# A two-block model step on one core: query copy, x store, scaling, Hadamard rounding and FFN banks put in other places

## The chip, the cores and the metric

The kernel runs on one core of a Trainium2 chip. The time is that of one execution on the device in microseconds (us); a run gives one such time, and the median of three runs is used.

## The reference

The input x is 4 x 512 tokens of 512 channels; a second tensor f has the same shape, cond is 4 x 128. Twice, with other constants (w, u), a tensor is scanned along the tokens (this goes by tile of 128 channels of one batch element):

```
a[t] = a[t-1] * decay + exp(min(f,30)) * f      (forwards and backwards)
b[t] = b[t-1] * decay + exp(min(f,30))
y = sigmoid(x) * num / max(den, 1e-8) * (0.8 + 0.2 * tf)
```

The first y feeds a segmented attention of 16 heads: q, k, v = y @ Wq, Wk, Wv (512 x 2048 each); per head and segment of 128 tokens a causal softmax attention, joined with a read from a memory matrix that a delta rule updates from segment to segment; then x = x + att @ Wo. The second y (from this new x) feeds a gated network: `hidden = silu(y @ W1) * (y @ W3)`, 2048 wide, a Walsh-Hadamard transform of hidden, and `x = x + hidden @ W2`. Everything is fp32.

## The kernel before

Channels lie on partitions, tokens in the free dimension. Products with weights are made from a high and a low part of each operand (fp32r): `three` (L543 to L548) issues three matmuls, high x high, high x low, low x high. A weight of 128 x 1024 enters in two halves through `stage`; ScalarE (L1366) or GpSimd (L1774) rounds it to the high part `wh`, GpSimd (L1776) or VectorE (`low_o`, L1041) subtracts for the low part `wl`. `weight_stream` sets the order of all weights, and six ring slots hold them. The second and later uses of the attention weights fetch the saved parts from memory.

Five engines run five programs written out by hand, `tensor`, `vector`, `scalar`, `gpsimd` and `sync`, which wait for each other through counting semaphores. An engine takes its program strictly in its order. Attention is a loop of 32 steps `n` (`NN`): a batch element times a pair of heads. In step n TensorE does in this order: `turn_k` (L665, transposed keys), `scores` (L677, into banks X[0], X[1]), `turn_att(n-1)` (L731), the value projection of step n+1 (`v_part`, into G[0], G[1]) with `update` and `recall` of the memory (L694, L702, L703, in Z) between, `turn_p` (L712), the key and query projections of step n+1 (`kq_part`, G), and `pv` (L722). Every fourth step from 4 on is a burst: it also applies Wo to the attention of four steps (`wo`, 8 weights), and `add_wo` (L1131) adds it into `xb`.

ScalarE copies what TensorE leaves in the banks: `copy_kq` (L1524) with `relu_kq` and `minus_exp` for keys and queries, `copy_kn` (L1557), the softmax exponentials `exp_s` (L1564), `copy_v` (L1549), `copy_pt` (L1572), `high_att` (L1581). `scores(n)` waits for both query copies of step n; the second of them, `copy_kq(n, "q", 1, G[1])`, stands at the head of ScalarE's step n. The first matmul of the key projection of head j waits for `copy_v` of half j (`a_v`), because it writes the bank from which the values are copied. `update(n, 1)` waits for `delta` and `t2` of VectorE's `recalled`.

Between this work each engine runs `behind(n, k)`, eight places per step, whose steps a table (`shared_out`, with the costs in `SCAN`, `HADAMARD` and `MODULATE`) hands out: the scans of later tiles (EK, EU, ER, yh on ScalarE; NF, DF, NBK, DBK and others on VectorE; EKV, EUV, ER, yl on GpSimd), and from step 23 on the transform of W2. The transform takes eight parts i: VectorE's levels in `HA`/`HB` (L989, L990), the rounding `HH` by ScalarE (`high_w2`, L1440), the rest `HL` by VectorE (`low_w2`, L995), two pairs of matmuls into X[0], X[1] (`hadamard`, L742 and L743, which wait for both and for the copies of part i-1), and the copies to `HO` by ScalarE (`out_w2`, L1458) with a store (L1460).

`keep_x1(b)` stores the finished `xb` of a batch element to `x1_s`, by four transfers of 256 KB from ScalarE's queue (L1601), in steps 9, 17 and 25 and once at the end. `fetch_x(b)` (L1989) on SyncE waits for it and loads the next element into `xb`. SyncE also issues all weight transfers, in order.

`scale_v` (L1839) on GpSimd multiplies the values of the next step; `split_w` is its weight splitting.

At the end of attention the network's units begin: 32 units `u` (`ffn`), each with a gate and a linear product of two heads j. `bank_of(u, k)` gives their banks: X for j = 0, G for j = 1; unit 0 is done inside step 31 in G[0], G[1]. VectorE's `gate` (L1137, L1142) frees a bank. Unit 1 stands between `turn_att(31)` and the last `wo(7)`:

```
            turn_att(NN - 1)
            w.wait_ge(v_jn, 8 * NN)
            up(1, 0, "1", bank_of(1, 0))
            up(1, 0, "3", bank_of(1, 1))
            for dc in range(NC):
                wo(7, dc)
```

`turn_att(n)` waits for `join(n, 3)` of VectorE (L1099, pT).

Of the kernel before, what the change touches and what calls it, by code (L numbers as in the profile page):

```python
# [238 lines left out]
def adaln_attn_ffn(nc, xT_d, fT_d, cond_d, wu_d, wq_d, wk_d, wv_d, wo_d, betas_d,  # L239
# [9 lines left out]
    with ExitStack() as ctx:  # L249
# [267 lines left out]
        def bank_of(u, k):  # L517

            return [X[0], X[1], G[0], G[1]][k]
# [22 lines left out]
        def tensor(e):  # L542
# [92 lines left out]
            def wo(m, dc):  # L635

                if dc == 0:
                    w.wait_ge(a_at, 8 * m + 8)
                    w.wait_ge(v_al, 8 * m + 8)
                if dc >= 2:  # L640
                    w.wait_ge(v_xb, 4 * m + dc - 1)
                elif m < 7:
                    w.wait_ge(a_v, 2 * (4 * m + 5) + dc - 1)
                else:
                    w.wait_ge(v_f3, 2)
                for half in range(2):
                    at = PLACE["o", 8 * m + 2 * dc + half]
                    hi, lo = ring(at)
                    wait_split(w, at)
                    for r in range(8):  # L650
                        cols = slice(128 * r, 128 * r + 128)
                        k = three(G[dc % 2][:, 0:256], hi[:, cols], lo[:, cols], ah[:, 8 * half + r, :],
                                  al[:, 8 * half + r, :], half == 0 and r == 0, half == 1 and r == 7)
                    k.then_inc(pe_o, 1)
# [120 lines left out]
            for n in range(NN):  # L775
# [56 lines left out]
                if burst:  # L832
                    kq_part(nx, "k", 1, 0)
                    kq_part(nx, "k", 1, 1)
                    for j in range(2):
                        kq_part(nx, "q", j, 0)
                        kq_part(nx, "q", j, 1)
                elif more:
                    kq_part(nx, "q", 0, 1)
                    kq_part(nx, "q", 1, 0)  # L840
                    kq_part(nx, "q", 1, 1)
            turn_att(NN - 1)
            w.wait_ge(v_jn, 8 * NN)
            up(1, 0, "1", bank_of(1, 0))
# [35 lines left out]
        def vector(e):  # L880
# [244 lines left out]
            def add_wo(m, dc):  # L1125
                b, half = m // 2, m % 2
                w.wait_ge(pe_o, 8 * m + 2 * dc + 2)
                w.wait_ge(d_xb[b], 16 if b == 0 else 64)
                src = G[dc % 2][:, 0:256].rearrange("p (h s r) -> p h s r", h=8, s=4)
                dst = xb[:, dc, :].rearrange("p (s h r) -> p h s r", s=4, h=16)[:, 8 * half:8 * half + 8]  # L1130
                e.tensor_tensor(dst, dst, src, ALU.add).then_inc(v_xb, 1)  # L1131
# [217 lines left out]
        def scalar(e):  # L1349
# [121 lines left out]
            def behind(n, k):  # L1471
                for name, i, _ in STEPS[at[0]:UPTO[n, k]]:
# [13 lines left out]
                    elif name == "hi":  # L1486
                        high_w2(i)
                    elif name == "load":
                        load_w2(i)
                    elif name == "mult":  # L1490
# [7 lines left out]
            def behind_ffn(u, k):  # L1498
                for name, t, _ in FSTEPS[late[0]:FUPTO.get((u, k), late[0])]:
# [10 lines left out]
                    elif name == "zh":  # L1510
                        w.wait_ge(v_zt, 4 * b + c + 1)
                        w.wait_ge(v_xb, 32)
                        w.wait_ge(d_x1[3], 64)
# [84 lines left out]
            def keep_x1(b):  # L1598
                w.wait_ge(v_xb, 8 * b + 8)
                for dc in range(NC):  # L1600
                    e.dma_start(x1_s[b, :, dc, :], xb[:, dc, :]).then_inc(d_x1[b], 16)  # L1601
# [54 lines left out]
            for n in range(NN):  # L1656
# [3 lines left out]
                if n > 0:  # L1660
                    copy_kq(n, "q", 1, G[1])
# [10 lines left out]
                if n > 1 and is_burst(n - 1) and (n - 1) // 4 % 2 == 0:  # L1672
                    keep_x1((n - 1) // 8 - 1)
# [21 lines left out]
                copy_pt(n)  # L1695
                if not more:
# [19 lines left out]
                if more:  # L1716
# [3 lines left out]
                    split_hi(here + (14 if burst else 6))  # L1720
                else:
# [33 lines left out]
        def gpsimd(e):  # L1755
# [104 lines left out]
            for n in range(NN):  # L1860
# [17 lines left out]
                if more:  # L1878
                    scale_v(nx)
                if burst:  # L1880
                    split_w(here + 11)
                behind(n, 6)
# [28 lines left out]
        def sync(e):  # L1911
# [53 lines left out]
            def z_load(b):  # L1965

                w.wait_ge(d_rs[b], 64)
                w.wait_ge(d_x1[b], 64)
# [17 lines left out]
            def fetch_x(b):  # L1986
                w.wait_ge(d_x1[b - 1], 64)
# [63 lines left out]
            def load_x(b):  # L2051
                w.wait_ge(d_x1[b], 64)
# [6 lines left out]
            def load_z(t):  # L2059
                if t < NT:  # L2060
                    _, b, c = TILES[t]
                    w.wait_ge(d_x1[b], 64)
# [92 lines left out]
```

## Time and profile before

| | us |
|---|---|
| median of 3 runs (1629.97 to 1631.04) | 1630.14 |
| the profiled execution, its own time | 1630.78 |
| its span | 1629.0 |
| TensorE busy | 1573.5 |
| VectorE busy | 1160.8 |
| ScalarE busy | 742.8 |
| GpSimd busy | 559.8 |

The profile is one execution. A row of the timeline gives start, duration, engine, line, operation, output<-inputs and shape; merged rows carry the number of instructions (x4) and the time of all. In brackets stands the idle time of the engine before it and what ended it. PE is TensorE's matmul, PEld its weight load, DVE VectorE, ACT ScalarE, POOL GpSimd, SP SyncE; ACTq and SPq are DMA issues of these. PEclk is the clock granted to TensorE as a share of full speed.

### The profile page before, as it was taken

How to read it: one execution, taken by the hardware profiler on the slowest of the kernel's cores; microseconds unless marked ns; L12 is line 12 of the kernel's file. 1: busy time of each engine (PE TensorE's matmuls, PEld its weight loads, DVE VectorE, ACT ScalarE, POOL GpSimd, SP SyncE). 2: the span in 40 equal slices, each digit the busy share in tenths (PEclk: the TensorE clock that was granted, in tenths of full speed). 3: DMA queues.
4: the chain of work that ended last, by engine and by line, in shares of the span. 5: the costliest groups of instructions: out<-in, count | busy, mean ns of one | idle time of the engine just before them, and what ended most of it. 6: DMA issues, size and time to landing. Idle time of an engine off the chain costs nothing.

```text
span 1629.0 us, 26858 instructions
## 1 busy us (share of the span) xinstructions
PE 1573.5 (97%) x9656; PEld 1396.4 (86%) x9656; DVE 1160.8 (71%) x2688; ACT 742.8 (46%) x1627; POOL 559.8 (34%) x408
## 2 busy tenths in 40 slices
PE   3799999999999999999999999999999999999999
PEld 2589989999999999999998899889888888888887
DVE  8988978888888878788765773666888884333333
ACT  3456556535635526536445653553554442222221
POOL 1665656242232122231102000134655553433431
PEclk9999999999999999999999999999999999999999
DMA  5356575595474475474477457238212214211101
GB/s 172 116 201 207 203 277 204 201 350 199 142 288 142 149 276 191 150 261 157 147 267 277 167 189 277 85 120 284 72 52 91 60 38 144 70 58 39 52 13 53
DMA packets 111252, 262.30 MB, mean 161 GB/s; under 512 B 11408, under 2 KB 36368, under 8 KB 110224
## 3 DMA queue, kind: packets, MB, share of 16 engines
q1 hardware_dynamic: 90240, 227.27, 39.3%
q10 hardware_dynamic: 20880, 33.31, 6.5%
q8 instruction: 78, 1.28, 0.3%
q14 instruction: 54, 0.44, 0.1%
HBM read 212.29 MB, written 48.25 MB: 160 GB/s over the span
## 4 chain that ended last, share of the span: by engine, by line
PE 84%; DVE 10%; issue 2%; ACT 2%; DMA 1%; ACTq 1%; DVEq 0%; SPq 0%
PE psG L546 16%; PE psG L548 16%; PE psG L547 16%; PE psX L722 3%; PE psX L547 3%; PE psX L546 3%; PE psX L548 3%; PE psX L677 3%; PE psZ L703 3%; PE psZ L694 2%; PE psZ L702 2%; PE psZ L547 2%; PE psY L547 2%; PE psZ L548 2%; PE psY L548 2%
## 5 line engine op out<-in xcount | busy, mean ns | idle before, releaser
L1776 POOL TENSOR_TENSOR wl<-stage,wh 128x512 fp32r<-128x512 f32 x160 | 226.4, 1437 | 166.2 <-ACT wh L1366 163.8
L546 PE MATMUL psG<-yh,wh 128*128 128x512 f32 x632 | 257.8, 408 | 4.4 <-ACT v L1549 2.5
L548 PE MATMUL psG<-yh,wl 128*128 128x512 f32 x632 | 247.6, 392 | 0.0
L547 PE MATMUL psG<-yl,wh 128*128 128x512 f32 x632 | 247.0, 391 | 0.0
L1839 POOL TENSOR_TENSOR vs<-v,omb 128x512 f32<-128x512 f32 x64 | 97.2, 1540 | 275.1 <-PE psX L722 272.0
L1846 POOL TENSOR_TENSOR hl<-sg,hh 128x512 fp32r<-128x512 f32 x64 | 86.4, 1350 | 220.6 <-ACT hh L1615 220.6
L546 PE MATMUL psG<-ah,wh 128*128 128x256 f32 x512 | 144.7, 283 | 1.1 <-DVE wl L1041 1.1
L547 PE MATMUL psG<-al,wh 128*128 128x256 f32 x512 | 142.9, 279 | 0.0
L548 PE MATMUL psG<-ah,wl 128*128 128x256 f32 x512 | 142.9, 279 | 0.0
L546 PE MATMUL psG<-wh,yh 128*128 128x256 f32 x480 | 142.0, 296 | 0.0
L546 PEld LDWEIGHTS psG<-yh,wh 128*128 128x128 f32 x632 | 119.5, 189 | 25.9 <-issue 3.2
L548 PEld LDWEIGHTS psG<-yh,wl 128*128 128x128 f32 x632 | 118.8, 188 | 26.1
L547 PEld LDWEIGHTS psG<-yl,wh 128*128 128x128 f32 x632 | 119.5, 189 | 20.1
L548 PE MATMUL psG<-wh,yl 128*128 128x256 f32 x480 | 136.1, 283 | 0.0
L547 PE MATMUL psG<-wl,yh 128*128 128x256 f32 x480 | 136.0, 283 | 0.0
L1366 ACT ACTIVATE wh<-stage 128x512 fp32r<-128x512 f32 x152 | 87.8, 622 | 91.6 <-PE psZ L548 29.0
L1615 ACT ACTIVATE hh<-sg 128x512 fp32r<-128x512 f32 x64 | 40.5, 632 | 174.6 <-DVE sg L1142 174.6
L1524 ACT ACTIVATE kT<-psG 128x512 f32<-128x512 f32 x62 | 37.0, 597 | 156.5 <-PE psG L548 156.5
L969 DVE RECIPROCAL DBK<-DF 128x128 f32<-128x128 f32 x120 | 107.3, 925 | 0.6
L1564 ACT ACTIVATE S<-S,st 128x128 f32<-128x128 f32 x256 | 99.1, 389 | 18.7 <-issue 13.9
L1051 DVE CUSTOM_DVE_ANT_0 S<-psX,mask 128x128 f32<-128x128 f32 x256 | 59.2, 286 | 57.6 <-PE psX L677 57.4
L546 PEld LDWEIGHTS psG<-ah,wh 128*128 128x128 f32 x512 | 96.3, 188 | 1.3 <-ACT wh L1366 1.2
(213 smaller groups left out, 4203.3 us busy)
## 6 DMA issues: line engine op xcount, KB each, us to landing
wh<-high_o SPq DMA_DIRECT2D x52, 512.0 KB, 3.5
wl<-low_o SPq DMA_DIRECT2D x52, 512.0 KB, 4.6
stage<-in_w SPq DMA_DIRECT2D x64, 256.0 KB, 4.3
wh<-high_k SPq DMA_DIRECT2D x23, 512.0 KB, 3.7
wl<-low_k SPq DMA_DIRECT2D x23, 512.0 KB, 4.8
wh<-high_q SPq DMA_DIRECT2D x23, 512.0 KB, 3.9
wl<-low_q SPq DMA_DIRECT2D x23, 512.0 KB, 5.6
wh<-high_v SPq DMA_DIRECT2D x22, 512.0 KB, 4.1
```

Source lines behind the costliest of these rows:

```text
L546: e.matmul(out, lh, rh, start=first, stop=False, skip_group_check=check)
L547: e.matmul(out, lh, rl, start=False, stop=False, skip_group_check=check)
L548: return e.matmul(out, ll, rh, start=False, stop=last, skip_group_check=check)
L677: m = e.matmul(X[j][:, seg(s)], qT[:, j, seg(s)], kT[:, j, seg(s)], start=True, stop=True)
L703: e.matmul(Z[j][:, 129:258], sq[:, j, seg(s)], mem[:, j, 0:P + 1], start=True, stop=True).then_inc(pe_am, 1)
L969: e.reciprocal(dbk[:, 128 * j:128 * j + 128], df[:, 128 * j:128 * j + 128]).then_inc(v_rc, 1)
L1051: m = e.tensor_tensor_reduce(S[:, j, seg(s)], X[j][:, seg(s)], mask[:, :], 1.0, NEG, ALU.add, ALU.max, st[:, 0, j, s:s + 1])
L1366: e.activation(hi, raw, ACT.Copy).then_inc(a_wh, 1)
L1564: m = e.activation(S[:, j, seg(s)], S[:, j, seg(s)], ACT.Exp, bias=st[:, 1, j, s:s + 1], scale=SCALE, accum_out=st[:, 2, j, s:s + 1])
L1776: e.tensor_tensor(lo, raw, hi, ALU.subtract).then_inc(p_wl, 1)
L1839: e.tensor_tensor(vs[:, :, j, :], v[n % 2][:, :, j, 0:P], omb[:, 128 * j:128 * j + 128].rearrange("p (a d) -> p a d", a=1).to_broadcast([P ...
L1846: e.tensor_tensor(hl[u % 2][:, j, :], hid(k)[:, :], hh[u % 2][:, j, :], ALU.subtract).then_inc(p_hl, 1)
```

## The change

It makes six edits.

- The copy of the second query head for step n+1 moves on ScalarE from the head of step n+1 to the end of step n, ahead of `behind(n, 7)`.
- `keep_x1` stores a batch element by one transfer of 1024 KB, not four, and in steps 9, 17 and 25 it stands behind `copy_pt`, not ahead of the softmax exponentials. All waits for `d_x1` count 16.
- In step 4 GpSimd's `scale_v` stands behind the splits of the weights up to `here + 11`.
- The part 7 of the transform of W2 is rounded (`high_w2(7)`) ahead of the copies `out_w2(6)` in step 30.
- Network units use G for j = 0 and X for j = 1. TensorE issues unit 1's first product into G[0] ahead of `turn_att(31)` and waits for `v_f1` there, for `v_f3` ahead of the second product.
- The last `wo(7)` and `add_wo(7)` use X.

```diff
--- before.py
+++ after.py
@@ -516,7 +516,7 @@
 
         def bank_of(u, k):
 
-            return [X[0], X[1], G[0], G[1]][k]
+            return [G[0], G[1], X[0], X[1]][k]
 
         def hid(k):
 
@@ -642,14 +642,14 @@
                 elif m < 7:
                     w.wait_ge(a_v, 2 * (4 * m + 5) + dc - 1)
                 else:
-                    w.wait_ge(v_f3, 2)
+                    w.wait_ge(v_jn, 8 * NN)
                 for half in range(2):
                     at = PLACE["o", 8 * m + 2 * dc + half]
                     hi, lo = ring(at)
                     wait_split(w, at)
                     for r in range(8):
                         cols = slice(128 * r, 128 * r + 128)
-                        k = three(G[dc % 2][:, 0:256], hi[:, cols], lo[:, cols], ah[:, 8 * half + r, :],
+                        k = three((G if m < 7 else X)[dc % 2][:, 0:256], hi[:, cols], lo[:, cols], ah[:, 8 * half + r, :],
                                   al[:, 8 * half + r, :], half == 0 and r == 0, half == 1 and r == 7)
                     k.then_inc(pe_o, 1)
 
@@ -839,9 +839,10 @@
                     kq_part(nx, "q", 0, 1)
                     kq_part(nx, "q", 1, 0)
                     kq_part(nx, "q", 1, 1)
+            w.wait_ge(v_f1, 2)
+            up(1, 0, "1", bank_of(1, 0))
             turn_att(NN - 1)
-            w.wait_ge(v_jn, 8 * NN)
-            up(1, 0, "1", bank_of(1, 0))
+            w.wait_ge(v_f3, 2)
             up(1, 0, "3", bank_of(1, 1))
             for dc in range(NC):
                 wo(7, dc)
@@ -1126,7 +1127,7 @@
                 b, half = m // 2, m % 2
                 w.wait_ge(pe_o, 8 * m + 2 * dc + 2)
                 w.wait_ge(d_xb[b], 16 if b == 0 else 64)
-                src = G[dc % 2][:, 0:256].rearrange("p (h s r) -> p h s r", h=8, s=4)
+                src = (G if m < 7 else X)[dc % 2][:, 0:256].rearrange("p (h s r) -> p h s r", h=8, s=4)
                 dst = xb[:, dc, :].rearrange("p (s h r) -> p h s r", s=4, h=16)[:, 8 * half:8 * half + 8]
                 e.tensor_tensor(dst, dst, src, ALU.add).then_inc(v_xb, 1)
 
@@ -1485,9 +1486,11 @@
                         keep_ratio(i)
                     elif name == "hi":
                         high_w2(i)
+                        if i == 7:
+                            out_w2(6)
                     elif name == "load":
                         load_w2(i)
-                    elif name == "mult":
+                    elif name == "mult" and i != 6:
                         out_w2(i)
                     elif name == "zsig":
                         z_sigmoid(i)
@@ -1510,7 +1513,7 @@
                     elif name == "zh":
                         w.wait_ge(v_zt, 4 * b + c + 1)
                         w.wait_ge(v_xb, 32)
-                        w.wait_ge(d_x1[3], 64)
+                        w.wait_ge(d_x1[3], 16)
                         e.activation(zh[b][:, c, :], ZS[t % 2][:, :], ACT.Copy).then_inc(a_zh, 1)
                 late[0] = FUPTO.get((u, k), late[0])
 
@@ -1597,8 +1600,7 @@
 
             def keep_x1(b):
                 w.wait_ge(v_xb, 8 * b + 8)
-                for dc in range(NC):
-                    e.dma_start(x1_s[b, :, dc, :], xb[:, dc, :]).then_inc(d_x1[b], 16)
+                e.dma_start(x1_s[b], xb[:, :, :]).then_inc(d_x1[b], 16)
 
             def sigmoid(u, j, bank):
                 k = 2 * u + j
@@ -1657,8 +1659,6 @@
                 nx, burst = n + 1, is_burst(n)
                 more = nx < NN
                 here = PLACE["v", nx] if more else PLACE["1", 0]
-                if n > 0:
-                    copy_kq(n, "q", 1, G[1])
                 copy_kn(n)
                 if n == 0:
                     copy_v(1, 0)
@@ -1669,8 +1669,6 @@
                     load_beta(n)
                 if more:
                     load_ombeta(nx)
-                if n > 1 and is_burst(n - 1) and (n - 1) // 4 % 2 == 0:
-                    keep_x1((n - 1) // 8 - 1)
                 behind(n, 0)
                 exp_s(n, 0)
                 split_hi(here + 3)
@@ -1693,6 +1691,8 @@
                 if burst:
                     split_hi(here + 6)
                 copy_pt(n)
+                if n > 1 and is_burst(n - 1) and (n - 1) // 4 % 2 == 0:
+                    keep_x1((n - 1) // 8 - 1)
                 if not more:
                     sigmoid(0, 1, G[0])
                 behind(n, 4)
@@ -1718,6 +1718,7 @@
                     copy_kq(nx, "q", 0, G[0])
                     exp_kq(nx, "q", 0, G[0])
                     split_hi(here + (14 if burst else 6))
+                    copy_kq(nx, "q", 1, G[1])
                 else:
                     high_h(0, 0)
                     high_h(0, 1)
@@ -1875,10 +1876,12 @@
                 behind(n, 4)
                 split_w(here + (9 if burst else 5))
                 behind(n, 5)
-                if more:
+                if more and n != 4:
                     scale_v(nx)
                 if burst:
                     split_w(here + 11)
+                if n == 4:
+                    scale_v(nx)
                 behind(n, 6)
                 if burst:
                     split_w(here + 13)
...
@@ -1984,7 +1987,7 @@
                 at[0] = UPTO[n, k]
 
             def fetch_x(b):
-                w.wait_ge(d_x1[b - 1], 64)
+                w.wait_ge(d_x1[b - 1], 16)
                 for dc in range(NC):
                     e.dma_start(xb[:, dc, :], xT_d[b, :, dc, :]).then_inc(d_xb[b], 16)
```

The other places with `d_x1` change in the same way.

ScalarE in step 25, from the load of the one-minus-betas to the copies of pT (x_s is the store of `xb`, S the exponentials, HO and HH the transform of W2, v the values), before:

```order
L1595 DMA omb<-beta_s 128x256
L1601 DMA x_s<-xb 128x512 x4
L1564 ACTIVATE S,st<-S,st 128x128 x8
L1458 ACTIVATE HO<-psX 128x512 x2
L1460 DMA w_s<-HO 128x1024
L1549 ACTIVATE v<-psG 128x4x128
L1440 ACTIVATE HH<-HA 128x1024
```

and now, with the copies of pT and the store that follows them:

```order
L1598 DMA omb<-beta_s 128x256
L1567 ACTIVATE S,st<-S,st 128x128 x8
L1459 ACTIVATE HO<-psX 128x512 x2
L1461 DMA w_s<-HO 128x1024
L1552 ACTIVATE v<-psG 128x4x128
L1441 ACTIVATE HH<-HA 128x1024
L1451 DMA HA<-in_w 128x1024
L1552 ACTIVATE v<-psG 128x4x128
L1575 ACTIVATE pT<-psY 128x512 x2
L1603 DMA x_s<-xb 128x2048
```

The four stores ahead of the exponentials are one store behind the copies of pT.

ScalarE in step 30, from the exponentials on, before:

```order
L1564 ACTIVATE S,st<-S,st 128x128 x8
L1458 ACTIVATE HO<-psX 128x512 x2
L1460 DMA w_s<-HO 128x1024
L1549 ACTIVATE v<-psG 128x4x128
L1440 ACTIVATE HH<-HA 128x1024
```

and now:

```order
L1567 ACTIVATE S,st<-S,st 128x128 x8
L1552 ACTIVATE v<-psG 128x4x128
L1441 ACTIVATE HH<-HA 128x1024
L1459 ACTIVATE HO<-psX 128x512 x2
L1461 DMA w_s<-HO 128x1024
```

The value copy and the rounding HH stand ahead of the two copies to HO and their store.

TensorE at the end of step 31 (mem is the memory, pT the joined attention), before:

```order
L703 MATMUL psZ<-mem,sq 128x129 x2
L731 MATMUL psY<-ident,pT 128x128 x8
L546 MATMUL psX<-yh,wh 128x512
L547 MATMUL psX<-yl,wh 128x512
L548 MATMUL psX<-yh,wl 128x512
```

and now (the first dots stand for three more such triples, those at the end for the second product in psG, which the last `wo` in psX follows):

```order
L703 MATMUL psZ<-mem,sq 128x129 x2
L546 MATMUL psG<-yh,wh 128x512
L547 MATMUL psG<-yl,wh 128x512
L548 MATMUL psG<-yh,wl 128x512
...
L731 MATMUL psY<-ident,pT 128x128 x8
L546 MATMUL psG<-yh,wh 128x512
...
```

Twelve matmuls of unit 1 stand between the last read of the memory and the last transposes.

## Rows read from the trace of the kernel before

**Rows 1.** The page, busy time by engine.
```profile
PE 1573.5 (97%) x9656; PEld 1396.4 (86%) x9656; DVE 1160.8 (71%) x2688; ACT 742.8 (46%) x1627; POOL 559.8 (34%) x408
```

**Rows 2.** TensorE's waits: engine, tile, line, releaser, us in total, times, longest.
```profile
PE psX L568 <- DVE oys L975: 28.6, 4, 22.5
...
PE psX L677 <- issue: 1.8, 1, 1.8
PE psG L546 <- DVE wl L1041: 1.1, 1, 1.1
```

**Rows 3.** Timeline, step 17: ScalarE's stores, TensorE's first key matmul.
```profile
616.90 2.94 ACTq L1601 DMA_DIRECT2D x_s<-xb  x4
...
624.23 0.47 PE L546 MATMUL psG<-yh,wh 128*128 128x512 f32 x1 [1.30 <-ACT v L1549]
```

**Rows 4.** Timeline, step 25: the same, and TensorE's memory update.
```profile
875.75 2.82 ACTq L1601 DMA_DIRECT2D x_s<-xb  x4
...
883.99 0.47 PE L546 MATMUL psG<-yh,wh 128*128 128x512 f32 x1 [1.15 <-ACT v L1549]
...
887.18 0.72 PE L694 MATMUL psZ<-delta,kn 128*128 128x129 f32 x4 [0.69 <-DVE t L1083]
```

**Rows 5.** Timeline, step 30: the transform's last two parts on three engines.
```profile
1042.87 1.06 ACT L1458 ACTIVATE HO<-psX 128x512 f32<-128x512 f32 x2
...
1044.33 0.60 ACT L1549 ACTIVATE v<-psG 128x512 f32<-128x512 f32 x1 [0.40 <-ACT HO L1458]
1044.82 1.05 ACT L1440 ACTIVATE HH<-HA 128x1024 fp32r<-128x1024 f32 x1
...
1045.90 1.22 DVE L995 TENSOR_TENSOR HL<-HA,HH 128x1024 fp32r<-128x1024 f32 x1 [3.44 <-ACT HH L1440]
...
1047.22 0.47 PE L742 MATMUL psX<-HH,had 128*128 128x512 f32 x1 [1.86 <-issue]
```

**Rows 6.** Stretches: busy us by engine (count), PEclk, DMA share, GB/s.
```profile
228.10:231.60 3.50, 3.50 (x31) 3.50 (x32) 3.40 (x20) 2.72 (x6) 3.33 (x4) 1.00 1.04 412
...
1048.60:1052.00 3.40, 3.40 (x15) 3.11 (x14) 0.00 (x0) 1.05 (x2) 0.91 (x1) 0.51 0.47 175
1091.00:1096.00 5.00, 5.00 (x24) 4.14 (x24) 1.98 (x3) 2.04 (x4) 1.29 (x1) 1.00 0.33 105
```

**Rows 7.** Timeline, end of step 31.
```profile
1080.64 5.80 POOL L1805 TENSOR_TENSOR yl<-zr,yh 128x512 fp32r<-128x512 f32 x4 [17.22 <-ACT yh L1469]
...
1090.01 1.09 PE L731 MATMUL psY<-ident,pT 128*128 128x128 f32 x8 [1.16 <-DVE pT L1099]
1090.13 0.68 DVE L1142 TENSOR_TENSOR sg<-psG,sg 128x512 f32<-128x512 f32 x1
```

**Rows 8.** Timeline, step 4: VectorE's low parts beside GpSimd's scaling.
```profile
200.04 3.00 POOL L1839 TENSOR_TENSOR vs<-v,omb 128x512 f32<-128x512 f32 x2 [1.86 <-PE psX L722]
...
200.51 3.09 DVE L1041 TENSOR_TENSOR wl<-stage,wh 128x512 fp32r<-128x512 f32 x2
...
205.16 2.48 DVE L1041 TENSOR_TENSOR wl<-stage,wh 128x512 fp32r<-128x512 f32 x4
```

**Rows 9.** Timeline, head of step 5, ScalarE and VectorE.
```profile
227.39 0.58 ACT L1524 ACTIVATE qT<-psG 128x512 f32<-128x512 f32 x1
...
234.57 0.48 DVE L1065 TENSOR_TENSOR mem<-psZ,mem 128x129 f32<-128x129 f32 x2
```

**Rows 10.** DMA issues by line: count, KB each, median us from issue to landing.
```profile
x<-x_s SPq DMA_DIRECT2D x4, 1024.0 KB, 6.6
```

**Rows 11.** Timeline, SyncE in step 9: the fetch, and the next weight.
```profile
371.23 2.50 SPq L1989 DMA_DIRECT2D xb<-in_xT  x4
376.72 0.33 SPq L1950 DMA_DIRECT2D wh<-high_k  x1
```

**Rows 12.** Timeline, ScalarE and TensorE at the head of step 17.
```profile
613.07 0.87 ACT L1557 ACTIVATE kn<-psY 128x384 f32<-128x384 f32 x2
...
614.82 0.82 PE L731 MATMUL psY<-ident,pT 128*128 128x128 f32 x6
```

More of the change, by code:

```diff
@@ L1967, in z_load @@
                 w.wait_ge(d_rs[b], 64)
-                w.wait_ge(d_x1[b], 64)
+                w.wait_ge(d_x1[b], 16)
                 w.wait_ge(pe_q, 2 * NG * (3 + b))
@@ L2051, in load_x @@
             def load_x(b):
-                w.wait_ge(d_x1[b], 64)
+                w.wait_ge(d_x1[b], 16)
                 if b >= 2:
@@ L2061, in load_z @@
                     _, b, c = TILES[t]
-                    w.wait_ge(d_x1[b], 64)
+                    w.wait_ge(d_x1[b], 16)
                     wait_attention(w)
```

## The prediction

> **What bounds the kernel now.** I read the page first: TensorE's matmuls are busy for 1573.5 of 1629.0 us [rows 1]. That leaves 55.5 us in which it stands still, and no edit here changes what it computes (the count of matmuls is the same). So the change can only be worth stalls of TensorE, and every other engine counts only where TensorE waits for it. The second view is the list of TensorE's waits [rows 2]. The largest, 28.6 us, is the opening, before the scans have given a first tile; nothing in the change touches it. What is left to win are single waits of 0.7 to 1.9 us, each in one step. I went through them in the timeline and asked of each which edit ends it, and what is late next.
>
> **Part by part.**
>
> The x store. ScalarE's queue issues four transfers in 2.94 us in step 17 [rows 3] and in 2.82 us in step 25 [rows 4], and the exponentials, the HO copies and the value copy `v` stand behind them in its order. TensorE's first key matmul may not write the bank before `v` is out of it, and idles 1.30 us [rows 3] and 1.15 us [rows 4] for it. In step 25 HH is behind `v` too, VectorE's HL behind HH, VectorE's `recalled` behind HL, and so the memory update idles 0.69 us more [rows 4]. With the stores behind `copy_pt` all of it comes 2.8 to 2.9 us earlier, more than each wait, so all three go: 1.30 + 1.15 + 0.69 = 3.14 us. Bounds: 0 if something else is late at the same place, 3.14 if nothing is. I take 3.14, since what else the first key matmul needs (weights, TensorE's own order) was there long before. One store is now issued while ScalarE copies pT and waits for the next key projection: cost nothing. In step 9 the store stood in the same place, and no wait of TensorE shows there: worth nothing. The last store, at the end of attention, is followed by network work that TensorE has queued: nothing.
>
> The last rounding. In step 30 ScalarE does the two HO copies of part 6 (1042.87) and issues their store, then `v` at 1044.33, then HH at 1044.82, then VectorE HL at 1045.90, and TensorE's Hadamard matmul starts at 1047.22 after 1.86 us of idle time [rows 5]. The change puts `v` first: it starts at 1042.87, and everything in the chain v, HH, HL, matmul comes 1044.33 - 1042.87 = 1.46 us earlier. The HO copies end then behind HH, at about 1045.4, still ahead of HL's end (1047.12 - 1.46 = 1045.7), so HL remains what comes last. Gain 1.46, idle time left 0.40.
>
> The clock. Behind that stall the granted clock is 0.51 of full speed, the 1.2 GHz level, from 1048.6 to 1052.0; after the stall of 1.8 us at the head of step 5 [rows 2] it stayed at 1.00 [rows 6]. The engine lost at most half of 3.4 us, 1.7 us; less, because a few weight loads and small matmuls do not run at the array's pace. I take 1.5 (bounds 0, if the level drops for another reason, and 1.7): a stall of 0.40 is far below every one that was followed by full speed. The Trainium skill's page "TensorE: Matmul & The Clock Gate", section "Why this matters for your kernels", warns only of idle gaps between matmul bursts that are longer than this one; by it the stall would not be the cause, the slow stretch could stay, and the sum would lose this term. The row, with 0.51 right behind the longest stall that I found in steps 4 to 31, speaks for the stall. This disagreement is a rival below.
>
> The second unit. TensorE's last transposes idle 1.16 us for pT [rows 7]. Now twelve matmuls of unit 1 stand ahead of them, whose bank G[0] is free since the gate of unit 0 and whose last input, `yl`, is done at 1080.64 + 5.80 = 1086.44 [rows 7]. In the next stretch 24 such matmuls, the first and the last in part, fill 5.0 us [rows 6], so twelve last some 2.7 us, more than the 1.16, which goes whole. What comes next: the second product needs the gate that starts at 1090.13 and lasts 0.68 us [rows 7]; it starts at 1090.01 - 1.16 = 1088.85, plus 2.7 and some 0.9 for the transposes: 1092.4, later than 1090.8. `wo(7)` needs the copies and low parts of both transposes, about 1.8 us behind them, and 2.7 us of matmuls cover that. Swapping X and G in all later units changes nothing: the waits are the same. Gain 1.16 (bounds 0 and 1.2).
>
> The scaling in step 4. GpSimd's `scale_v` runs from 200.04 to 203.04, and beside it VectorE's two low parts take 3.09 us; four of the same later take 2.48 us, 0.62 each [rows 8]. TensorE waits 1.1 us for the slower ones [rows 2]. Without the neighbour they take 1.24 and the wait goes.
>
> The query copy, with it. At the head of step 5 the second query copy starts at 227.39, behind a scan exponential that waits for VectorE, and the scores idle 1.8 us [rows 2, 9]. Ahead of it, the copy starts as soon as the projection ends, some 2.5 us earlier. But TensorE's next need of VectorE is the memory add at 234.57 [rows 9], on which the next read of the memory follows at once, and VectorE is busy for 3.40 of 3.50 us in the stretch behind the stall [rows 6]; it has no idle time by which it could come earlier. So TensorE, 1.8 us earlier, waits the 1.8 us there. These two edits together are worth what VectorE gains by step 5. It gains at most 3.09 - 1.24 = 1.85 us in step 4, but the moved scaling now runs beside its scans and key sums before step 5 and takes some of it back. Bounds: 0, and 1.1 + 1.8 = 2.9. I take 0.9, near the lower wait. In the other steps where scan work stood ahead of the query copy (12 of them) the copy waited for the projection anyway.
>
> What the query copy costs. In these steps one scan operation of 0.6 to 0.7 us now runs behind the copy, not while ScalarE waits for TensorE, and `copy_kn` comes later by so much. In step 17 it lasts until 613.94, and `turn_att` that waits for it starts at 614.82 [rows 12]: 0.88 us of cover, enough for 0.7. Only in step 24 (HH and a small copy, some 1.3 us) is it used up; half of the two copies is enough for the first transposes, and I put 0.1 us there, within the rounding.
>
> Sum: 3.14 + 1.46 + 1.5 + 1.16 + 0.9 = 8.16 us. The profiled execution's own time is 1630.78, so 1622.6. It stands 0.64 above the median of 1630.14, and each wait that goes whole gives a little more than its idle time, since the profile counts it from a modelled end of the matmul before. I therefore forecast **1622.0 us**, 0.5% faster. A measurement of this kernel can tell about 0.2%, 3.3 us, from no change: 1626.9 is the border.
>
> **Rivals.**
>
> - The clock falls in another place, or the level was not bound to the stall (the page's reading): 8.16 - 1.5 = 6.7 us, 1623.5. For it: one occurrence is thin evidence, and a stall of 1.8 us left the clock alone. Chance 0.15.
> - Step 5 gives back its stall whole, because VectorE runs ahead without its neighbour: 2.0 us more, 1620.0. Against it: VectorE's row of work without a pause. Chance 0.10.
> - The moved scan operations land on TensorE's path. If the cover of 0.88 us [rows 12] is used up elsewhere, each of 12 steps costs up to 0.6: 7 us, 1629.2, no difference that can be told. It decides once an operation is longer than the cover. Against it: the operations that I see are shorter. Chance 0.07.
> - Slower: the single store. Landing took 6.6 us for 1024 KB in the median [rows 10]. In step 9 SyncE fetches the next element at 371.23 and issues a key weight at 376.72 [rows 11]. A store issued behind `copy_pt` shortly before, at 370, and landing 6.6 us later, or 10 us (half as much again, for other traffic), would let the fetch start at 376.6 to 380, and its four issues of 2.50 us [rows 11] put the weight at 379.1 to 382.5, up to 5.8 us late; three times 5.8 on TensorE's path is 17.4 us: 1639.4. It decides where a weight is used within that time of its issue. Against it: this weight goes into a slot of six that is read two steps (52 us) later. Chance 0.03.
> - The change does not do what it says: the order of the instructions shows each move. Half of the stalls return for reasons that I do not see: 1626.0, chance 0.05.
>
> My forecast has 0.60.
>
> **How the numbers follow.** The range takes in the first two rivals and the bounds of the terms: low 1619.5 (2.9 in place of 0.9, and 0.5 of run to run), high 1625.5 (no clock term, and 2 us of stalls that return). It leaves out the third, fourth and most of the last, 0.15 in all. Faster by over 0.2%: 0.60 + 0.15 + 0.10 + 0.03 = 0.88; slower by over 0.2%: 0.03; the rest, 0.09, is within 0.2%.
>
> **What would show it.** In the profile after: TensorE's waits for v in steps 17 and 25 and for t2 in step 25 are gone; the Hadamard matmul of step 30 idles some 0.4 us and no stretch of half clock follows it; the last transposes do not idle; the wait of 1.1 us in step 4 is gone, and that of 1.8 us in step 5 is no longer at the scores but at `copy_kn` and at the memory read, 0.9 us less in sum over steps 4 and 5. The forecast is wrong if a wait for weights or for `copy_kn` appears in many steps, or if TensorE's idle time falls by less than 4 us.

## The result, and the profile after

The changed kernel takes **1621.1 us** (median of 4 runs, 1620.47 to 1621.25); the kernel before took 1630.59 in the same session (4 runs). The ratio is 0.994, 95% interval 0.9925 to 0.9954. That is 9.5 us or 0.6% faster; the forecast was 1622.0, from 1619.5 to 1625.5.

The page of the changed kernel, span and busy time by engine:

```profile
span 1619.3 us, 26845 instructions
...
PE 1570.0 (97%) x9656; PEld 1393.9 (86%) x9656; DVE 1157.1 (71%) x2688; ACT 742.8 (46%) x1627; POOL 560.2 (35%) x408
```

The number of matmuls is the same, and TensorE stands still for 49.3 us in place of 55.5 [rows 1]. It is also busy for 3.5 us less, with the same work. A third profile of the kernel before, shown below, whose clock fell nowhere that it cost, is busy for 1571.5 us; so some 2.0 of the 3.5 us are the clock, and the rest may be idle time that the modelled ends of the matmuls hide. TensorE's waits in the changed kernel (tile, line, releaser: us in total, times, longest):

```profile
PE psX L568 <- DVE oys L976: 30.9, 4, 22.7
PE psZ L702 <- DVE mem L1066: 5.1, 5, 2.2
PE psZ L703 <- DVE mem L1066: 3.1, 7, 0.5
PE psG L546 <- DMA wl<-low_q: 1.8, 1, 1.8
PE psY L731 <- ACT kn L1560: 1.7, 1, 1.7
...
PE psX L742 <- DVE HL L996: 0.4, 1, 0.4
```

Against the list of before [rows 2]: gone are the waits for `v` (steps 17 and 25), for the low part in step 4, for pT at the end of attention, and the 1.8 us at the scores of step 5. The Hadamard matmul of step 30 idles 0.4 us. New is a wait of 1.7 us for `kn`, and the wait for low_q, a weight of step 8 that the change does not touch, is 1.8 us (1.3 before).

For the account I cut TensorE's trace at the first matmul of each step's scores. In all fourteen profiles of this document a step's length repeats within 0.06 us in most steps; steps 0, 4, 5, 8, 17, 25 and 30 and the stretch from 31 on do not repeat so well, and once (in the second profile of the kernel before) step 24 took 0.87 us more. For these steps several profiles are needed. The steps that differ, in the first profiles of both kernels (us):

```
step                 before    after    less by
0                     28.36    26.64     1.72
4 and 5               79.17    78.82     0.35
8                     50.29    50.77    -0.48
17                    27.84    26.32     1.52
25                    30.35    28.01     2.34
30                    31.78    28.77     3.01
31 to the last matmul 557.43  556.11     1.32
```

The other steps add 0.1 us, and the first scores come 0.17 us later; the sum is the 9.7 us of the spans. Nothing was forecast for the first row and the third.

In step 30 VectorE's HL and TensorE's Hadamard matmul follow the rounding at once (ScalarE, changed kernel):

```profile
1037.47 0.58 ACT L1552 ACTIVATE v<-psG 128x512 f32<-128x512 f32 x1
1037.94 1.05 ACT L1441 ACTIVATE HH<-HA 128x1024 fp32r<-128x1024 f32 x1
1038.89 1.06 ACT L1459 ACTIVATE HO<-psX 128x512 f32<-128x512 f32 x2
```

`v` has no idle time ahead of it now, and the HO copies run beside HL; before, they stood ahead of both [rows 5].

At the end of attention twelve matmuls stand ahead of the last transposes, which start without an idle time (TensorE, first and last of the twelve):

```profile
1080.16 0.48 PE L546 MATMUL psG<-yh,wh 128*128 128x512 f32 x1
...
1082.75 0.39 PE L548 MATMUL psG<-yh,wl 128*128 128x512 f32 x1
1082.98 1.03 PE L731 MATMUL psY<-ident,pT 128*128 128x128 f32 x8
```

### The profile page after: what moved, and what is told of

Same layout as the page of the kernel before. It is cut to its first block, busy times and chain, and to the rows that moved or that the text cites. A ratio compares the mean times of both kernels' runs of the same rounds, so it can differ in the third digit from the quotient of the medians.

```text
span 1619.3 us, 26845 instructions
## 1 busy us (share of the span) xinstructions
PE 1570.0 (97%) x9656; PEld 1393.9 (86%) x9656; DVE 1157.1 (71%) x2688; ACT 742.8 (46%) x1627; POOL 560.2 (35%) x408
## 4 chain that ended last, share of the span: by engine, by line
PE 85%; DVE 10%; issue 2%; DMA 2%; ACT 1%; SPq 0%; POOL 0%; ACTq 0%; DVEq 0%; POOLq 0%
PE psG L546 15%; PE psG L548 15%; PE psG L547 15%; PE psX L546 3%; PE psX L547 3%; PE psX L548 3%; PE psX L722 3%; PE psX L677 3%; PE psZ L703 3%; PE psZ L694 2%; PE psZ L702 2%; PE psZ L548 2%; PE psZ L547 2%; PE psY L547 2%; PE psY L548 2%
## 5 line engine op out<-in xcount | busy, mean ns | idle before, releaser
L546 PE MATMUL psG<-ah,wh 128*128 128x256 f32 x448 | 126.7, 283 | 0.0
L547 PE MATMUL psG<-al,wh 128*128 128x256 f32 x448 | 125.1, 279 | 0.0
L548 PE MATMUL psG<-ah,wl 128*128 128x256 f32 x448 | 125.1, 279 | 0.0
L546 PEld LDWEIGHTS psG<-wh,yh 128*128 128x128 f32 x480 | 91.6, 191 | 0.3
```

What stands on the lines that cost most here:

```text
L546: e.matmul(out, lh, rh, start=first, stop=False, skip_group_check=check)
L547: e.matmul(out, lh, rl, start=False, stop=False, skip_group_check=check)
L548: return e.matmul(out, ll, rh, start=False, stop=last, skip_group_check=check)
```

## Experiments

### The query copy and the scaling

Three variants of the changed kernel: the query copy back at the head of the step (first edit), the scaling back ahead of the splits (second), and both. Their expectations follow in this order.

```diff
+                if n > 0:
+                    copy_kq(n, "q", 1, G[1])
                 copy_kn(n)
...
-                    copy_kq(nx, "q", 1, G[1])
```

```diff
-                if more and n != 4:
+                if more:
                     scale_v(nx)
                 if burst:
                     split_w(here + 11)
-                if n == 4:
-                    scale_v(nx)
```

> The changed kernel with the second query copy back at the head of the step. In the changed kernel step 5 has two stalls of TensorE, 1.7 us at the last transposes for copy_kn and one at the memory read (1.3 us longer from start to start than without a wait). Theory: both are set by VectorE's unbroken row of work, so the copy's place is worth nothing there: with it back the scores of step 5 wait some 1.8 us, the memory read waits again as long as in the changed kernel or less, and the scores of step 6 start within 0.3 us of the changed kernel's 252.0 us. In all other steps nothing moves. Time 1621 +- 0.5, unless the half-clock stretch of the opening falls elsewhere (1.7 us). Rival: the query copy is worth its wait; the scores of step 6 then start 1 us or more later, 1622.5.

> The changed kernel with GpSimd's scaling of step 4 back ahead of the splits. Theory: the wait of 1.1 us for the low part in step 4 returns, and step 5 gives most of it back, since VectorE then works without its neighbour there: steps 4 and 5 together are 0.2 to 0.6 us longer than in the changed kernel, and of that step 8's wait for the weight low_q takes the rest, since that weight's landing hangs on transfers. Time 1621.1 to 1621.7. Rival (as I forecast it for the two edits): 0.9 us or more stay, 1622.0.

> The changed kernel with both of these undone. Theory: steps 4 and 5 are 0.35 us longer in sum (the difference of the two traces), step 8's wait for low_q is 0.5 us shorter again, so that from step 9 on the two edits together are worth nothing: 1621.1 +- 0.4 at the same opening. If the opening's half-clock stretch comes from the moved query copy it returns to 79 us and costs 1.7: 1622.8. Rival: the two edits are worth the 0.9 that I forecast, 1622.0, with step 9's start 0.9 later.

Measured: 1619.72 us (1619.24 to 1620.58), 1623.09 (1620.27 to 1624.78) and 1621.38 (1620.56 to 1622.5), beside 1629.62 for the kernel before (14 runs, 1626.93 to 1632.23). The second lies above both its theory and its rival, but its five runs spread over 4.5 us, and its profiled run took 1620.49. With such a spread the medians cannot tell a microsecond, and the steps are the better witness:

```
us                  step 4   step 5    sum    step 8
before               50.48    28.69   79.17    50.29
both back            50.48    28.67   79.15    50.29
scaling back         50.46    28.71   79.17    50.00
query copy back      48.94    29.60   78.54    50.09
changed              49.15    29.67   78.82    50.77
```

The query copy is worth nothing here: with it back the sum is not longer. The wait only changes its place. With the copy late, the scores wait 2.7 us and the memory read not at all; with it early, `kn` takes 1.7 us and the memory read the rest. Two lines of TensorE's waits, with the copy back:

```profile
PE psZ L702 <- DVE mem L1066: 3.9, 4, 2.2
PE psX L677 <- issue: 2.7, 1, 2.7
```

The memory read's waits sum to 3.9 us, where the changed kernel has 5.1. VectorE's row of work sets the end of both, so I had the mechanism right and the size of the first wait too small (1.8 expected).

The scaling is worth 0.35 us in the pair of first profiles and 0.6 between the last two variants. Over all profiles of this document it is 0.6: with the scaling moved, steps 4 and 5 last 78.03 to 78.82 us (eight profiles, mean 78.48), without 78.84 to 79.17 (six, mean 79.11). In step 4 it gives all that was forecast: the two low parts that took 3.09 us beside GpSimd [rows 8] take 1.29 us now (first row below), the four behind them 2.59 (2.48 before), and the step is 1.3 to 1.8 us shorter. But the scaling now falls beside VectorE's key sums of step 5 (VectorE and GpSimd, changed kernel):

```profile
198.91 1.29 DVE L1042 TENSOR_TENSOR wl<-stage,wh 128x512 fp32r<-128x512 f32 x2
...
201.75 2.59 DVE L1042 TENSOR_TENSOR wl<-stage,wh 128x512 fp32r<-128x512 f32 x4
```

```profile
217.26 2.72 DVE L1123 SCALAR_TENSOR_TENSOR sk<-kT,etmp 128x512 f32<-128x512 f32 x2
```

```profile
214.94 3.48 POOL L1840 TENSOR_TENSOR vs<-v,omb 128x512 f32<-128x512 f32 x2
218.36 1.08 POOL L1796 TENSOR_SCALAR ER<-ER 128x512 f32<-128x512 f32 x1
```

One such sum takes 0.68 us without a neighbour, two would be 1.36; they took 2.72, the first beside the scaling, the second beside the operation behind it, and step 5 is 0.7 to 1.0 us longer.

Step 8, with its wait for low_q, is not tied to these edits: it lasted 49.80 to 50.77 us in all profiles, both ways (the last version below, which moves that weight, left out). And step 0 lasted 26.6 us in all three variants, also with the copy back; the changed kernel's gain of 1.72 us there is not the query copy's.

### The rounding alone

The kernel before with this single edit:

```diff
                         high_w2(i)
+                        if i == 7:
+                            out_w2(6)
...
-                    elif name == "mult":
+                    elif name == "mult" and i != 6:
                         out_w2(i)
```

> The kernel before with the last rounding ahead of the copies as the only change. Theory: the Hadamard matmul of step 30 idles some 0.4 us in place of 1.86, and the stretch of half clock behind it is gone: 1630.6 - 1.46 - 1.5 = 1627.6, and step 30 lasts 28.8 us (31.8 before). Rival (the level of the clock does not hang on that stall): the half-clock stretch stays somewhere in steps 29 to 31, 1629.1, step 30 or its neighbour 30.3 us.

1626.93 us (10 runs, 1625.5 to 1627.99), beside 1629.62: ratio 0.9984, interval 0.9974 to 0.9993. The median gain, 2.7 us, is near the theory's, but the profile shows that not all went as the theory has it. Step 30 lasts 30.07 us, there is no stretch of half clock, and the Hadamard matmul still idles 1.7 us. ScalarE was held up at another place, by the issue of a small load ahead of the exponentials:

```profile
1036.93 1.75 ACTq L1597 DMA_DIRECT2D omb<-beta_s  x1
```

At the same place the issue took 0.44 us in the kernel before and 0.45 in the changed kernel. So this profile has a stall of the old length without the drop of the clock. That put in doubt that the stall is what takes the clock down, and the next three kernels are for that.

### Stalls of other lengths, and the clock

The changed kernel with the rounding back behind the copies, and with one or two more copies of HA ahead of the rounding:

```diff
+                if i == 7:
+                    for m in range(2):
+                        e.activation(HH[:, :], HA[i % 2][:, :], ACT.Copy).then_inc(a_had, 1)
+                        w.wait_ge(a_had, m + 2)
                 e.activation(HH[:, :], HA[i % 2][:, :], ACT.Copy).then_inc(a_h, 1)
```

> The changed kernel with the last rounding of the W2 transform back behind the copies. The stall ahead of the Hadamard matmul in step 30 is some 1.85 us again, in a kernel where everything else is the changed one. Theory (a stall so long takes the clock down): half clock behind it, step 30 lasts 31.8 us, 1624.1. Rival, for which the run with the rounding alone spoke (a stall of 1.7 us and no half clock): the level does not hang on the length of this stall, step 30 lasts 30.2 us, 1622.6.

> The changed kernel with one more copy of HA to HH (1.05 us, and a wait for it) ahead of the rounding of part 7, which makes the stall ahead of the Hadamard matmul 1.5 us in place of 0.4. Both theories: no half clock (the stalls of 1.7 and 1.8 us had none), step 30 lasts 29.9 us, 1622.2.

> The same with two more copies: a stall of 2.6 us. Theory (length decides, somewhere above 1.7 us): half clock behind it, 1.5 to 1.7 us on top, step 30 lasts 32.5 to 32.7 us. Rival (length does not decide alone): none, step 30 lasts 31.0 us.

1621.33 us (1620.78 to 1623.29), 1622.02 (1621.54 to 1625.68) and 1623.23 (1622.56 to 1625.51), beside 1630.25 for the kernel before (13 runs). The stalls ahead of the Hadamard matmul were 1.9, 2.7 and 3.3 us (the small load's issue took 1.70 us in the second and 1.21 in the third), step 30 lasted 30.27, 31.11 and 31.73 us, and no half clock followed in any of them. With the longest:

```profile
1042.30 0.47 PE L742 MATMUL psX<-HH,had 128*128 128x512 f32 x1 [3.33 <-DVE HL L996]
```

```profile
1042.00:1045.40 3.40, 3.10 (x19) 2.86 (x20) 1.44 (x7) 1.92 (x4) 2.29 (x2) 1.00 0.38 154
```

The third figure from the right is the granted clock, 1.00. So the length of the stall alone does not decide. The Trainium skill's page "TensorE: Matmul & The Clock Gate", section "Why this matters for your kernels", asks for no idle gaps of TensorE above about 3 us, or the level falls. The rows here do not agree with it: a stall of 3.33 us, just above that figure, left the level alone, and behind one of 1.86 us [rows 5, 6], well below it, the level fell.

### The kernel before, two more profiles

> The kernel before once more, for a second profile. So far its one profile has a half-clock stretch behind the stall of 1.86 us in step 30, and none of the four variants with stalls of 1.7 to 3.3 us at that place has one. Theory (a stall there makes the drop possible, and chance decides where in the run the level falls): step 30 lasts 30.2 us in some profiles of this kernel and 31.8 in others. Rival (it belongs to this kernel at this place): 31.8 us each time. Likewise for the opening: step 0 lasts 28.4 us in the first profile and 26.6 in most variants; by chance, either; as the kernel's property, 28.4.

> The kernel before for a third profile, with the same two theories on steps 0 and 30: 26.6 or 28.4 us and 30.2 or 31.8 us if chance decides, 28.4 and 31.8 us if it is this kernel's.

1629.31 us (8 runs, 1628.23 to 1635.18; the profiled one 1628.83) and 1626.99 (one run). Both have the stall of 1.9 us (1.86 and 1.92). The stretches behind it, in the second and in the third profile:

```profile
1046.50:1049.90 3.40, 3.40 (x16) 3.20 (x15) 0.23 (x1) 1.44 (x3) 1.36 (x2) 0.50 0.38 154
```

```profile
1045.50:1048.90 3.40, 3.40 (x24) 3.05 (x23) 0.32 (x2) 1.59 (x3) 1.47 (x2) 1.00 0.49 158
```

One program, one stall, and the clock falls in one execution and not in the other: step 30 lasts 31.77 and 30.31 us. The drop costs 1.47 us where it comes (31.77 - 30.31), the size that I took, but it does not come each time. Step 0 shows the same: 26.66 and 26.64 us here, 28.36 in the first profile. In that one the level was low from 79.2 to 82.7 us, on TensorE's full row of matmuls; in twelve of the fourteen it fell 7 to 10 us earlier, at 69.6 to 71.8 us, where TensorE waits soon after in any case. There the slow matmuls cost nothing: in the changed kernel the wait behind them, for the memory read at 78.5 us, is 1.18 us long, where the first profile of before has 2.09 and one of 0.46 more ahead of it. Only in one of the twelve, where the level stayed low for 6.8 us (the rounding undone), did step 0 take 0.7 us more (27.39). The two places:

```profile
79.20:82.70 3.50, 3.50 (x20) 3.50 (x18) 2.81 (x9) 0.27 (x1) 3.42 (x3) 0.51 0.88 322
```

```profile
71.50:75.00 3.50, 3.50 (x13) 2.80 (x13) 3.47 (x13) 3.20 (x13) 1.20 (x2) 0.51 0.58 233
```

The first is the kernel before, the second the changed kernel. The variant with one more copy, otherwise as the changed kernel there, had the late drop and 28.38 us too. So the 1.72 us of step 0 are not this kernel's property, and whether a given pair of profiles shows the 1.47 of step 30 differs from execution to execution.

Two profiles more say little on how often the level falls, but the record has the mean granted clock of every run. It is 0.9961 over 42 runs of the kernel before, 0.9972 over 25 runs of the changed kernel and its variants with the short stall, 0.9971 over the 10 of the rounding alone, and 0.9971 over the 14 of the three variants with the long stall (standard errors of some 0.0002). The difference of 0.0011 is 1.7 us of full clock per execution, as much as one stretch of 3.4 us at half level. So the kernel before does lose more to the clock, by about one drop. But undoing the rounding in the changed kernel does not bring that loss back, so the stall of step 30 alone is not its cause. Where the level fell in the runs without a kept trace is not on record.

### The store's place

The single store back ahead of the exponentials (ScalarE's program), in the changed kernel:

```diff
                     load_ombeta(nx)
+                if n > 1 and is_burst(n - 1) and (n - 1) // 4 % 2 == 0:
+                    keep_x1((n - 1) // 8 - 1)
                 behind(n, 0)
...
                 copy_pt(n)
-                if n > 1 and is_burst(n - 1) and (n - 1) // 4 % 2 == 0:
-                    keep_x1((n - 1) // 8 - 1)
```

> The changed kernel with its single x store put back ahead of the exponentials. Theory: the place is not needed. Four issues took 2.94 us, one takes a quarter, some 0.7; the wait of 1.3 us in step 17 needs at least 2.94 - 1.30 = 1.6 us of issues in the way, so nothing of it returns: step 17 lasts 26.3 us and step 25 28.0, as in the changed kernel, 1621.1 +- 0.7. Rival: the issue of 1024 KB takes as long as the four together; then steps 17 and 25 last 27.8 and 30.3 us again, 1624.9.

1620.51 us (1619.78 to 1621.81). Steps 17 and 25 last 26.32 and 27.99 us, as in the changed kernel. The issue in step 17:

```profile
614.23 0.44 ACTq L1603 DMA_DIRECT2D x_s<-xb  x1
```

0.44 us, where four issues took 2.94 [rows 3], and 2.20 to 2.67 in three other profiles. The one transfer gives the whole gain; the new place adds nothing to it. Four transfers at the new place were not run, so whether the place alone would have done is open.

### The network's second unit

The banks and the order of unit 1 as before, in the changed kernel (the last `wo` and `add_wo` are in G again too):

```diff
-            return [G[0], G[1], X[0], X[1]][k]
+            return [X[0], X[1], G[0], G[1]][k]
...
-            w.wait_ge(v_f1, 2)
-            up(1, 0, "1", bank_of(1, 0))
             turn_att(NN - 1)
-            w.wait_ge(v_f3, 2)
+            w.wait_ge(v_jn, 8 * NN)
+            up(1, 0, "1", bank_of(1, 0))
             up(1, 0, "3", bank_of(1, 1))
```

> The changed kernel with the network's banks and the order of unit 1 as before. Theory: the wait of 1.2 us ahead of the last transposes returns and nothing else; from the scores of step 31 to the last matmul 1.2 us more than in the changed kernel (there 555.4 to 556.9 in the runs so far), 1622.3. Rival: another wait (the gates, the last projection) took its place in the changed kernel, so that the way back costs under 0.5 us.

1621.8 us (1620.51 to 1623.11). The wait returns:

```profile
PE psY L731 <- DVE pT L1099: 1.2, 1, 1.2
```

Step 31 to the last matmul lasts 556.75 us, with no other wait of note behind it; five variants of the changed kernel without this wait or a late gate took 555.4 to 555.5, so the edit is worth 1.3. The other four profiles of the changed order took 555.97 to 556.91 us, so the stretch scatters by as much as the edit is worth; in three of these, the changed kernel's own among them, a gate of the network came 0.4 to 0.5 us late, as it did in two profiles of the kernel before.

### A version that beats both

Two of the waits that are left have plain causes. In steps 23, 25, 26, 27 and 29 the memory add for the last read stands behind the joins of segment 1 on VectorE. In step 8 the query weight's load stands behind four pairs of saves on SyncE:

```profile
338.26 1.12 SPq L1953 DMA_DIRECT2D wh<-high_q  x1
339.42 1.15 SPq L1954 DMA_DIRECT2D wl<-low_q  x1
```

```diff
+                early = not is_burst(n) and n > 22
+                if early:
+                    memory(n, 2)
                 join(n, 1)
...
-                memory(n, 2)
+                if not early:
+                    memory(n, 2)
                 join(n, 2)
...
+                if n == 8:
+                    keep(here + 7)
+                    load_w(here + 11)
                 if burst:
                     keep(here + 9)
                     load_w(here + 12)
```

> The changed kernel with two more edits. VectorE adds the memory (for the last read) ahead of the joins of segment 1 in the non-burst steps from 23 on, where TensorE waits 0.68 us each in steps 23, 25, 26, 27 and 29; and SyncE issues step 8's query weight behind two of the four pairs of saves, not behind all four, which ends the wait of 1.0 to 2.0 us for low_q. Theory: steps 25, 26, 27 last 27.4 us in place of 28.0, step 8 48.8 in place of 49.8 to 50.8: 5 x 0.6 + 1.5 = 4.5 us, 1616.6. Rival: the moved saves make the next weights late (v or k of step 10), so that step 9 or 10 loses what step 8 gains, 1618; or the joins, now later, hold up TensorE at a bank, and the five steps gain nothing, 1619.6.

**1616.03 us** (5 runs, 1615.2 to 1617.44), beside 1628.92 for the kernel before (15 runs): ratio 0.9922, interval 0.991 to 0.9935. The load is issued 6 us earlier:

```profile
331.85 1.55 SPq L1957 DMA_DIRECT2D wh<-high_q  x1
```

Step 8 lasts 48.68 us, as a burst without waits does, and steps 9 and 10 are unchanged. Steps 23, 25, 26, 27 and 29 are each 0.50 to 0.53 us shorter, 2.6 in sum (3.0 expected); step 8 gives 2.1 against the changed kernel's first profile. The changed kernel itself was not run beside it, so the distance between the two is known from the ratios to the kernel before and from the steps alone. The waits at the last read fall from 3.1 us to

```profile
PE psZ L703 <- DVE mem L1066: 0.5, 2, 0.3
```

## Why the prediction was right, and where it was not

**What bounds the kernel.** Right: what was gained is stalls of TensorE and its clock; the other engines' busy times moved by 3.7 us at most (VectorE's, 1160.8 to 1157.1).

**The x store, 3.14.** Mechanism right, size low: steps 17 and 25 gave 1.52 + 2.34 = 3.86 us. Against the second and third profile of the kernel before it is 3.45 and 3.16 us. The steps gave some 0.7 us more than the idle times that the profile lists, in each of the three pairs; those start at a modelled end of the matmul before, which would hide some 0.2 us in each of three waits. I had said so and gave this term nothing for it. The gain also hangs on how long the four issues happen to take: step 17 was 27.84, 27.47 and 27.49 us in three profiles of the kernel before. I put the gain down to the place behind `copy_pt`; the experiment says that the single transfer is enough, at either place.

**The last rounding, 1.46.** Right. Without the drop of the clock step 30 lasted 30.31 us before and 30.27 with the edit undone; in the changed kernel 28.77, 1.5 less, and the idle time left is the 0.4 that I worked out.

**The clock, 1.5.** Size right (1.47), reason wrong. I read from one occurrence that a stall of that length takes the level down, and that a shorter one would not. Two of the three profiles of the kernel before have the drop and one has none, at stalls of 1.86 to 1.92 us; stalls of 1.7 to 3.3 us in four variants had none. The seven profiles with a wait of 0.4 to 0.8 us there had none either, so that a stall makes the drop possible fits all, but none of seven against two of seven is too few to call it shown. On the average of many runs the kernel before did lose 1.7 us more of full clock than the changed one, so there is a loss of this size; but the variants with the stall put back did not have it. What decides stays open.

**The second unit, 1.16.** Right: 1.2 us of wait, 1.3 of time, and no wait in its place.

**The scaling and the query copy, 0.9.** The reasoning held: VectorE's gain in step 4 comes through, the wait of step 5 only moves to `copy_kn` and the memory read, and the scaling takes part back. The step that failed is the size of what it takes back: I named it and allowed 0.9 to 1.0 for it in sum, and of a gain of 1.33 in step 4 it took 0.98 in step 5, which left 0.35 here (0.6 on the average of all profiles). The nearest row, low parts at 1.5 in place of 0.62 us beside the same scaling [rows 8], would have priced it: two key sums at 1.36 in place of 0.68.

**What I did not forecast.** 1.72 us at the opening came by chance, -0.48 in step 8 too. In this pair of profiles they, and the store term that was too low, more than make up for the 0.9 that was too high: 8.16 forecast, 9.7 measured. A pair without drops that cost anything, the third profile of before against the changed kernel's, differs by 1625.2 - 1619.3 = 5.9 us. Many runs show the middle: the medians of all runs are 1629.42 us (before, 42 runs) and 1620.88 (the changed kernel and its variants with the short stall, 25 runs), 8.5 us apart. The steps give 0.6 + 3.2 to 3.9 + 1.5 + 1.3 = 6.6 to 7.3 us for the stalls, and the mean clock at most 1.7 more. So the sum of 8.16 was good on the average, but its clock term was met by luck, since the mechanism behind it was wrong.

**The rivals.** The clock staying as it was would have been 1623.5; the rival's reason, that the level is not bound to the stall, fits the runs better than mine. Step 5 does not give back its stall whole. The moved scan operations cost nothing: all steps from 9 to 16 and 18 to 24 are unchanged within 0.05 us. The late store cost nothing either, but not because it was early. In step 9 it was issued at 368.0 and landed 7.2 us later; the fetch waited for it, and the weight behind the fetch was issued at 377.05, where it was 376.72 before [rows 11]. Since step 9 now starts 1.4 us earlier, that is 1.8 us later in the step, and the two steps until the weight's use took it up:

```profile
375.25 1.76 SPq L1992 DMA_DIRECT2D xb<-in_xT  x4
377.05 0.43 SPq L1953 DMA_DIRECT2D wh<-high_k  x1
```

## What to carry to other kernels

Add up single waits of the engine that bounds, each traced to its releaser and to what is late next; that gave each part here within three quarters of a microsecond. Before a term rests on a drop of the clock, or a gain is read from one pair of profiles, take more profiles of the same kernel, and the mean granted clock of many runs: here one program differed from itself by 1.5 us in one step and by 1.7 in another. And a wait that moves to the next instruction of the same late engine is worth nothing, however large it stands in the list; the work in that engine's row has to shrink.

## What the runs showed that I had not expected

The stretches of half clock fall at different places in executions of the same program, at the opening and in step 30, and what they cost hangs on the place: 1.7 us on a full row of matmuls, nothing where TensorE waits soon after. One 1024 KB store is issued on ScalarE's queue in 0.33 to 0.45 us, four of 256 KB in 1.90 to 2.94. The issue of one small load of 128x256, in step 30, took 0.44 to 0.52 us in ten profiles and 0.83, 1.21, 1.70 and 1.75 in four others at the same place of the program, and what stands behind it is late by so much. Beside GpSimd's multiplication VectorE's low parts took 1.5 us in place of 0.65; its two key sums, beside the multiplication and the GpSimd operation that followed, took 2.72 in place of 1.36.
